# First chunk's features in two halves, the output projection in half-precision parts, and new places for the steps of four bodies

## The reference, cut to what matters

```python
x_proj = inputs @ w_in + b_in
x1 = conv_general_dilated(inputs, dw_kernel, ...) + dw_bias          # depthwise 3x3
x1 = gelu(layernorm(x1) * ln_gamma + ln_beta)
offset = (x1 @ w_off + b_off).reshape(B, H, W, G, K2, 2)             # G = 8 groups, K2 = 9 taps
mask = softmax((x1 @ w_mask + b_mask).reshape(B, H, W, G, K2), axis=-1)
samp = _bilinear_gather(xg, pxf, pyf, Hp, Wp)                        # 4 corners of each tap
out = jnp.sum(samp * maskg[..., None], axis=4)
...
return out @ w_out + b_out
# then x = x + conv(ln(x)); router: softmax over 8 experts, the best 2 kept
h = gelu(einsum('end,edh->enh', xe, W1) + b1); y = einsum('enh,ehd->end', h, W2) + b2
out = (weights[:, :, None] * sel).sum(axis=1)                        # t = t + ffn(ln(t))
```

## Time and profile before

| | |
|---|---|
| runs | 282.99, 280.44, 283.21 us, median 282.99 |
| profiled execution | 281.17 us, span 279.3 us |
| granted TensorE clock, mean | 0.987 of full speed |
| busy share of the span | PE 93%, DVE 81%, ACT 68%, POOL 43% |

### The profile page before, as it was taken

The page is one execution under the profiler, slowest core; times in us unless marked ns, Lnnn a source line. Parts: engine busy times, 40 slices in busy tenths (PEclk is TensorE's granted clock), DMA queues, the critical chain, the costliest instruction groups (busy, mean ns, idle before and its releaser), DMA issues.

```text
span 279.3 us, 8247 instructions
## 1 busy us (share of the span) xinstructions
PE 259.9 (93%) x3312; PEld 173.0 (62%) x3312; DVE 226.2 (81%) x680; ACT 188.8 (68%) x351; POOL 118.8 (43%) x123
## 2 busy tenths in 40 slices
PE   7983999999869999999999999999998999987894
PEld 2550567565547776744677777545897987755462
DVE  5999999999978889998896976999969644476464
ACT  3777565747855678979766748997656676733563
POOL 6140011945060861410597435001986691249440
PEclk9998699999999999999999999999999999999999
DMA  5940000000000000000000000000000000000000
GB/s 148 286 110 0 2 1 5 1 2 2 1 3 2 4 5 2 0 2 0 2 11 12 2 4 2 2 0 0 4 21 2 4 2 2 0 2 2 18 2 19
DMA packets 7187, 4.83 MB, mean 17 GB/s; under 512 B 5089, under 2 KB 6830, under 8 KB 7086
## 3 DMA queue, kind: packets, MB, share of 16 engines
q1 hardware_dynamic: 7150, 4.31, 6.2%
HBM read 2.04 MB, written 0.52 MB: 9 GB/s over the span
## 4 chain that ended last, share of the span: by engine, by line
PE 79%; DVE 10%; POOL 4%; issue 3%; ACT 2%; DMA 1%; DVEq 0%; POOLq 0%; ACTq 0%
PE z_ps L1546 8%; PE z_ps L1548 8%; PE ga_ps L1578 8%; PE ga_ps L1580 7%; PE ga_ps L1579 7%; PE m_ps L1663 5%; PE z_ps L1560 5%; PE m_ps L1680 3%; PE m_ps L1641 3%; PE m_ps L1642 2%; PE m_ps L1525 2%; PE m_ps L1647 2%; PE m_ps L1470 2%; PE m_ps L1649 2%; PE m_ps L1692 2%
## 5 line engine op out<-in xcount | busy, mean ns | idle before, releaser
L1305 ACT ACTIVATE wk<-z_ps 128x512 int32<-128x512 f32 x108 | 64.3, 601 | 35.1 <-PE z_ps L1548 34.9
L890 DVE TENSOR_TENSOR prod<-ga_ps,wx 128x480 f32<-128x480 f32 x96 | 61.6, 651 | 20.3 <-PE ga_ps L1580 19.8
L1578 PE MATMUL ga_ps<-v_all,wk 128*128 128x80 f16 x576 | 76.5, 202 | 1.3 <-DVE prod L890 0.9
L1579 PE MATMUL ga_ps<-v_all,wk 128*128 128x80 f16 x576 | 76.5, 202 | 0.0
L1580 PE MATMUL ga_ps<-v_all,wk 128*128 128x80 f16 x576 | 76.5, 202 | 0.0
L565 POOL TENSOR_TENSOR prod<-prod 128x960 f32<-128x960 f32 (+1 forms) x20 | 38.6, 1930 | 85.9 <-DVE prod L890 85.9
L1578 PEld LDWEIGHTS ga_ps<-v_all,wk 128*128 128x128 f16 x576 | 56.6, 99 | 28.0 <-ACT wk L1305 10.9
L1579 PEld LDWEIGHTS ga_ps<-v_all,wk 128*128 128x128 f16 x576 | 57.2, 99 | 6.6
L1580 PEld LDWEIGHTS ga_ps<-v_all,wk 128*128 128x128 f16 x576 | 57.4, 100 | 0.0
L1546 PE MATMUL z_ps<-tab,sel_hi 128*128 128x512 f16 x108 | 41.5, 384 | 2.1 <-issue 2.1
L1336 ACT ACTIVATE h_all<-m_ps 128x512 f32<-128x512 f32 x64 | 36.6, 610 | 9.6 <-PE m_ps L1649 8.7
(11 more groups left out here) (279 smaller groups left out, 564.2 us busy)
## 6 DMA issues: line engine op xcount, KB each, us to landing
v_all<-still SPq DMA_DIRECT2D x1, 1440.0 KB, 10.5
h_all<-in_W SPq DMA_DIRECT2D x1, 512.0 KB
w_s<-in_W SPq DMA_DIRECT2D x1, 512.0 KB
x_tok<-in_x SPq DMA_DIRECT2D x1, 384.0 KB, 6.0
out_dram<-x_tok SPq DMA_DIRECT2D x6, 64.0 KB, 1.8
w_high<-w_high SPq DMA_DIRECT2D x1, 256.0 KB, 3.1
const<-in_table SPq DMA_DIRECT2D x1, 218.0 KB, 2.7
vec<-in_vectors SPq DMA_DIRECT2D x1, 132.5 KB
```

Of the source, the lines that this page charges most:

```text
L890: dve.tensor_tensor(prod[q % 2][:].rearrange("p k n -> p (k n)")[:, f * PB * NV:(f + 1) * PB * NV] .rearrange("p (n c l) -> p n c l", n=PB ...
L1305: act.activation(wk[n % WR][:], z_ps[use % 2][:], ACT.Relu, scale=HIGH_UNIT * FINE / Z_UNIT).then_inc(s_wk, 1)
L1578: pe.matmul(to, w_h, high, start=True, stop=False)
L1579: pe.matmul(to, w_h, low, start=False, stop=False)
```

## The change

It has four parts.

- The features of chunk 0 are made in two halves (pairs of groups 0 and 1, then 2 and 3). The prologue makes the first half; the second half's steps and its part of the table move into body 0 (`first_rows`, `first_table` and others). For this `feat` and the flat arrays change their layout to group pair before tile, and `column_weights` is split into one instruction for each pair of groups (8 in the last chunk).
- The prologue's order is new: convolution before projection, `conv_norm` before `project_low`, half of `selections` moved ahead of the first norm, two coefficients moved to ACT, all 18 `sel_lo` copies on ACT, the 8 `bias_product` moved there from body 0 in place of zero matmuls. `normalise` waits for POOL's factor after the subtraction and not ahead of it.
- The output projection uses half-precision high and low parts: `samples_out` writes the high part, a new DVE step `samples_low` the low part, and `project_out` has three matmuls of half precision for each tile. Five DVE instructions prepare the weights in `router_parts`.
- The places are new. `input_stats` and `input_norm` of a chunk stand one body later, `router_parts`, `bias_rows` and half of `low_w1` stand in body 1, ACT's `high_w1` in body 0. PE's wait for the experts' weights stands ahead of the first `expert_in`. The zero matmuls in bodies 0 and 3 are gone.

```diff
-PE_FIRST = {"input_t": 6.5, "convolve": [10, 10.5, 10.5, 10.5], ... "zeros": [32, 34, 31]}
+PE_FIRST = {"input_t": 7, "convolve": [12.5, 14.5, 15.5, 12.5], ... "b2": 0, "first_table": 16}
-FILL = [9, 2, 9, 13, 7, 6, 2]
+FILL = [9, 2, 9, 2]
+FILL_BIAS = [1, 2, 2, 2, 3, 3, 3, 3]
...
+def features_done(a, part=None):
+    return part + 1 if a == 0 else a + 2
...
-            def normalise(dst, src, mv, rstd, done, half=None):
+            def normalise(dst, src, mv, rstd, scaled, count, done, half=None):
...
-                link(dve.tensor_tensor(dst[:, t, :], src[:, t, :], mv[:, t, 0:1].to_broadcast(whole), ALU.subtract))
+                n_c = mark(dve.tensor_tensor(dst[:, t, :], src[:, t, :], mv[:, t, 0:1].to_broadcast(whole), ALU.subtract))
+                dve.wait_ge(scaled, count)
+                dve.wait_ge(s_chain, n_c)
...
+            def samples_low(d, half=None):
+                n = tokens_of(half)
+                dve.wait_ge(s_sth, d + 1 + (half or 0))
+                dve.scalar_tensor_tensor(samp_both[C:P, n], half_ps(1, half)[0:C, n], -1.0 / W_UNIT, samp_both[0:C, n],
+                                         ALU.mult, ALU.subtract).then_inc(s_st, 1)
...
                     if j == 0:
-                        if n == at["second_norm"]:
-                            input_norm(1)
-                    if j + 2 < CHUNKS:
+                        if n == at["first_logits"]:
+                            tap_logits(0, 1)
+                        if n == at["first_rows"][0]:
+                            clamps(0, 1)
...
+                    if has_a:
                         if n == at["input_stats"]:
-                            input_stats(j + 2)
+                            input_stats(j + 1)
...
             def project_out(d, half=None):
                 pe.wait_ge(s_st, d + 1 + (half or 0))
...
-                    ins = pe.matmul(projected(half)[:, t * C:(t + 1) * C], samp_t[:, t * P:(t + 1) * P], w_out_s,
-                                    start=True, stop=True)
+                    to, sample = projected(half)[:, t * C:(t + 1) * C], samp_both[:, t * P:(t + 1) * P]
+                    pe.matmul(to, sample, w_out_both[:, 0, :], start=True, stop=False)
+                    pe.matmul(to, sample, w_out_both[:, 1, :], start=False, stop=False)
+                    ins = pe.matmul(to, ones[:], w_out_both[:, 2, :], start=False, stop=True)
...
+            def bias_products(first, zeros):
+                for e, n in enumerate(zeros, first):
+                    keep_clock(ga_ps[0][:], n)
+                    bias_product(e)
...
             for t in range(TP):
                 convolve(0, t)
-            keep_clock(ga_ps[0][:], FILL[3])
+            pe.wait_ge(s_winl, 1)
+            project(0)
+            bias_products(0, FILL_BIAS[0:3])
+            conv_t(0)
+            bias_products(3, FILL_BIAS[3:4])
+            pe.wait_ge(s_ones, 1)
+            offsets(0)
...
+            bias_products(4, FILL_BIAS[4:8])
             pe.wait_ge(s_dist, 1)
...
-            pe.wait_ge(s_sel, 3)
+            keep_clock(ga_ps[0][:], FILL[3])
+            features_t(0, 0)
+            pe.wait_ge(s_sel, 2)
             for j in range(CHUNKS):
-                if j == 1:
-                    pe.wait_ge(s_w1, E)
-                    pe.wait_ge(s_w1d, (2 * E + 1) * 16)
-                    pe.wait_ge(s_zero, 3)
                 body(j, j + 1 < CHUNKS, j > 0)
```

More of the change, by code:

```diff
@@ L47 @@
 TAP_SCALE = 2.0 ** 6
+OUT_SCALE = 2.0 ** 6
+ONES = 2.0 ** 3
 NR = 97
@@ L70 @@
-DVE_FIRST = {"input_stats": 10.5, "input_norm": 16, "input_low": 6.5, "conv_stats": 9.5, "project_low": 8.5, "conv_norm": 13,
-             "image_out": 14.5, "positions": [17, 20, 23.5], "rows": [21, 21.5, 27.5, 31], "edges": 17.5, "hats": 32.5,
-             "tap_weights": [31.5, 35.5], "lane_sum": [16, 16, 23.5, 24.5, 31, 35, 3, 5], "residual": 10, "inner_norm": 32.5,
-             "zn_low": 17, "route": [18, 23, 25.5], "expert_weights": 26, "b2": 2.5, "bias_rows": 27, "router_parts": 8,
-             "w1_low": [3.5, 4.5, 8, 8], "outputs_in": [30.5, 26.5], "second_stats_": 25, "second_norm": 3.5}
@@ L95 @@
-DVE_THIRD = {"input_stats": 0, "input_norm": 19.5, "input_low": 5, "conv_stats": 18.5, "project_low": 13, "conv_norm": 21.5,
-             "image_out": 21, "positions": [24, 27, 24], "rows": [28, 28.5, 29.5, 29.5], "edges": 27, "hats": 31,
-             "tap_weights": [31, 31.5], "lane_sum": [11.5, 16, 20.5, 27.5, 30, 33, 0, 3], "residual": 9, "inner_norm": 14,
-             "zn_low": 16.5, "route": [19, 21.5, 25], "expert_weights": 26, "b2": 25.5, "bias_rows": 5, "router_parts": 0,
-             "w1_low": [4, 7, 9.5, 15.5], "outputs_in": [33.5, 35]}
@@ new lines @@
+DVE_FIRST = {"samples_low": 10, "input_stats": 0.5, "input_norm": 3, "input_low": 9, "conv_stats": 16, "project_low": 13,
+             "conv_norm": 17.5, "image_out": 20.5, "positions": [25, 25.5, 25], "rows": [28, 28, 31, 32], "edges": 31.5,
+             "hats": 34, "tap_weights": [35, 35.5], "lane_sum": [16.5, 17, 24, 24.5, 34, 35, 3, 5], "residual": 10,
+             "inner_norm": 32.5, "zn_low": 17, "route": [18, 23, 25.5], "expert_weights": 26, "b2": 1.5, "bias_rows": 35,
+             "router_parts": 23, "w1_low": [14.5, 20.5, 35.5, 35.5], "outputs_in": [30.5, 26.5], "second_stats": 0,
+             "second_norm": 4.5, "first_logits": 7, "first_rows": [3.5, 4.5, 4.5, 11.5, 12], "first_edges": 11.5,
+             "first_hats": 14.5, "first_weights": [13, 15.5]}
@@ new lines @@
+DVE_THIRD = {"samples_low": 8, "input_stats": 4.5, "input_norm": 6, "input_low": 10, "conv_stats": 19.5, "project_low": 19,
+             "conv_norm": 21.5, "image_out": 23, "positions": [26, 26.5, 26], "rows": [26.5, 26.5, 29.5, 30], "edges": 29.5,
+             "hats": 34, "tap_weights": [32, 34], "lane_sum": [15, 17, 24.5, 24.5, 29, 33, 0, 3], "residual": 11.5,
+             "inner_norm": 16, "zn_low": 18.5, "route": [19.5, 23.5, 33.5], "expert_weights": 34, "b2": 25.5, "bias_rows": 5,
+             "router_parts": 0, "w1_low": [4, 7, 9.5, 15.5], "outputs_in": [35, 35.5]}
@@ L104 @@
-           47.5, 49, 54, 55.5, 56.5, 60.5, 60.5, 61, 61, 61.5, 63, 64.5, 65, 65], "expert_out": [50.5, 60.5, 61, 64.5, 69,
-           70.5, 71.5, 71.5], "outputs_t": [66, 71.5], "b2": 0.5, "half_samples_t": 69, "half_project_out": 69,
-           "half_experts_t": 71.5, "half_router": 71.5, "zeros": [18, 32]}
+           "table": [45.5, 47.5], "samples_t": 12.5, "project_out": 23.5, "experts_t": 36, "router": 43, "expert_in": [47.5,
+           49, 49.5, 52.5, 53, 53.5, 55.5, 55.5, 56, 56.5, 58, 58.5, 60, 60.5, 61, 61], "expert_out": [53, 53, 60, 60.5,
@@ L1172, in body @@
                             router_parts()
[L1173 to L1175 removed]
+                    for q in range(E // 2):
+                        if j == q // 2 and n == at["w1_low"][q]:
+                            low_w1(q)
                     for m in range(FILLS):
```

508 lines of the change are left out of this document (288 added, 220 removed).

## The result

The changed kernel takes 282.37 us (median of 20 runs, 282.19 to 282.67), the kernel before 280.90 (20 runs beside it, 280.43 to 283.21). The ratio is 1.0035, with a 95% interval of 1.0018 to 1.0052: slower by a third of a per cent, which is within the 1% that I called no change. I had forecast 279.8, a gain of 0.8%. That number stood on 281.95 for the kernel before, which its 20 runs put at 280.90; as a difference, -2.2 us was forecast and +1.5 measured. The profiled execution has a span of 280.8 us against 279.3.

What follows compares the result with a forecast made beforehand. DVE was taken to bound body 0 and PE bodies 1 and 2. The terms -0.4 + 0.9 - 0.56 - 2.1 + 0 made -2.2 us, from 281.95 to 279.8 us; range 275.5 to 284.0.

Steps and rivals of the forecast that it cites:

- body 2: Third whole-chunk stage: DVE's work rises from 49.7 to 52.9 us, PE stays ahead, 0.56 us gained.
- the tail: Kernel's end: POOL's longer list offset by an earlier half, 0 us (-0.5 to +2); as rival +2.0, chance 0.09.
- DVE becomes the bound: Rival for bodies 1 and 2: DVE's idle time cannot be filled, costing 5.2 and 3.2 us; 287.9 us, chance 0.15.
- body 1: Stage after chunk 1's column weights: DVE's work reaches 53.4 us, 0.9 us lost; bounds -0.56 and +5.2.
- body 3: Last body: zero matmuls, projection time and a 0.47 us wait go, 2.1 us gained, or 1.2.
- The prologue: Start of the kernel: reordering lets DVE enter body 0 at 30.5 instead of 33.97 us, PE at 27.7 instead of 31.4.
- Body 0: First body, bound by DVE: 52.1 us of work plus 1.8 idle, ending at 84.4 against 84.82, 0.4 us gained.
- my bound of -2.2: Largest gain allowed for body 0: with no DVE idle time it would end at 82.6 us.
- The hole of 2.13 us: PE's wait at 79.23, head of body 1, for the experts' bias transfers: it goes, paying only through DVE's column weights.
- the rival of the bound: Another wording for "DVE becomes the bound", chance 0.15; if only body 1 behaves so, 284.1 us.
- Bodies 1 and 2 and the projection: Half-precision projection: PE's 0.92 us a chunk becomes 0.36, 0.56 saved; DVE gets low-part and weight work.
- The clock: Rival: the granted clock falls once ahead of body 1, PE loses 3.4 us of pace; 283.2 us, chance 0.04.

Runs made afterwards that it cites:

- e1: Changed kernel, with POOL in body 2 waiting for DVE's normalising products before it starts the tap trees next in its queue: 279.40 us, ratio 0.9915.
- e9: Kernel of e1 plus ten one-element memsets on DVE in body 3, to move the fetch of instructions: 278.95 us, ratio 0.9894.
- e10: Kernel before, plus seventy one-element memsets on DVE in body 3, making 832 instructions as in the changed kernel: 282.69 us, ratio 1.0027.
- e11: Kernel before, plus eighty one-element memsets on DVE in body 3, as control for e10: 281.82 us, ratio 1.0011.
- e4: Changed kernel, plus two scratch memsets on DVE between prologue and body 0, so DVE enters body 0 late: 287.10 us, ratio 1.0197.
- e13: Kernel of e9 without the five DVE instructions for the projection's weight parts (output incomplete), five more empty memsets instead: 277.36 us, ratio 0.9872.
- e5: Kernel of e1 with the weight parts (router_parts) at place 8.5 of body 1 instead of 5: 283.32 us, ratio 1.0074.
- e12: Kernel of e9 with body 1's output projection at place 14, its weight parts at 10, and following steps later: 280.69 us, ratio 0.9968.
- e14: Kernel of e9 with ACT's two exponentials of body 1 at place 29 instead of 28: 280.92 us, ratio 1.0008.
- e2: Changed kernel with the output projection in fp32 again, without DVE's low part, weight instructions kept: 282.39 us, ratio 1.0026.
- e6: Kernel of e1 with the fp32 output projection of e2: 279.58 us, ratio 0.9937.
- e3: Changed kernel plus eight products of zeros on PE at the end of body 0, to hold the clock: 282.43 us, ratio 1.0016.

## Why the prediction was wrong

*The step that failed* is body 2: "DVE gets [...] 52.9 of 57.0, 93%. PE stays ahead: -0.56". The amount was right: DVE has 53.8 us there in e1, 2.1 of them in the two later stands. What I left out is that two of DVE's instructions can be as long as POOL's. Body 2 took 2.70 us more instead of 0.56 less, and e1 gives 2.97 us of the whole back. I looked at POOL's order only in the tail, and there only at the length of its list; which of POOL's instructions would run beside which of DVE's I never asked. The section on the cores says that the engines meet only at semaphores; DVE and POOL met here without one. None of my rivals had this mechanism. "DVE becomes the bound" came nearest in its price for body 2 (3.2), but it blamed amount. And the -0.56 itself didn't show: without the first two stands body 2 takes 57.60 us, as before.

*Luck.* The total is off by 3.7 us (+1.5 for -2.2) only because the errors offset each other: +3.3 in body 2, +2.7 in body 1 and +1.1 at the end, against -2.5 up to the column weights of chunk 1, -0.6 in body 3 and -0.3 in the tail.

*What I had no term for.* The last landing is 1.1 us longer, because DVE has more instructions (738 on the page against 680) and a packet of instructions falls into it. The rows of e1 and e9, and of e10 and e11, show it with 0.8 and 0.7 us.

*The prologue* came as worked out: `conv_stats` at 12.13 (forecast 12.2), half-size instructions of 0.30 and 0.23 us, DVE in body 0 at 30.28 (30.5), PE's first table product there at 27.58 (27.7). *Body 0* was mis-sized, in the other direction. I had 52.1 us of work on DVE and 1.8 idle; it has 50.41 and 1.25, so the weights of chunk 1 are ready at 81.94, not 84.4. Of the 1.7 us of work too much, 0.6 is the second half, whose steps take 8.4 us there and not 9.0. The other 1.1 is a set of statistics: I called them even, but the stage of the kernel before holds two sets (33.88, and 47.78 to 48.91), and that of the changed kernel one (30.32). The term is -2.88, not -0.4, and lay outside my bound of -2.2. e4 shows that the entry is worth its full size. The hole of 2.13 us is gone, as forecast.

*Body 1* took 3.58 us more where I had 0.9, inside the bounds that I gave (up to 5.2). DVE's work is 54.1 us (forecast 53.4), but PE stands for 3.4 us. Of these 0.8 are at 83.6, for a `weigh` at the head of the body, 1.5 at 89.8, behind the weight parts, where e13 shows that DVE's amount counts, and 1.1 at 123.7, for ACT:
```profile
121.79 1.28 ACT L1425 ACT_TABLE_LOAD   x1 [1.15 <-PE m_ps L1792]
123.08 1.08 ACT L1425 ACTIVATE h_all<-m_ps 128x512 f32<-128x512 f32 x2
```
So for 2.3 us it is the rival of the bound, at two places. I took a mean share of busy time (96%) for a whole body, though its head is not like the rest: from 82.0 to 90.2 PE is busy 5.89 of 8.20 us and DVE 7.74, after which PE hardly waits. e5, e12 and e14 found no better place for parts and exponentials. That the amount is the cause at 89.8 is shown; whether another order of the whole body could hide it stays open.

*Bodies 1 and 2 and the projection.* It costs PE 0.36 us a chunk as forecast (four tiles 0.09 apart at 91.32). My terms for it (0.56 for PE in each of three bodies, 0.3 in the last half, less 0.2 in the tail) make 1.8 us; up to DVE's end it measures 0.65 (e2) to 0.9 us (e6), and the five weight instructions, for which I had 0.9 us of DVE's work, cost 1.24 (e13). *Body 3* gave 2.70 (forecast 2.1); no run splits it. *The tail* to DVE's end gave 0.3, so POOL's longer list cost nothing. *The clock* fell ahead of body 1 as in the rival, for 3.4 us, and cost nothing (e3) where the rival had 3.4.

With POOL's waits and the ten empty instructions the kernel takes 278.95 us, 1.2% under the changed kernel and 1.06% (0.74 to 1.39) under the one before. It is the fastest whole version here.

## What to carry to other kernels

When instructions of DVE and POOL are re-placed, look at what stands next in the other engine's queue: where DVE's instruction reads two inputs from SBUF, the POOL instruction that releases it should not be followed by a long one that is ready. Two waits of half a microsecond were worth three here. In these runs a stand cost where PE then had nothing to do, so read PE's idle rows first and DVE's long rows second. And when a change of computing and a change of time don't agree, cut the trace at the last compute instruction: what follows it (here a fetch of instructions in the last transfer) may be the difference. And a part of a change is priced with its preparations: taking out the low part alone made the projection look like a gain.
